# Bias products of the next step's first half issued before the wait for its queries and keys

## What is computed

```python
scores = einsum('bhqd,bhkd->bhqk', q, k) * scale      # 16 heads of 8 features
# attention 0: scores += -log(distances + 1e-9) * abs(distance_scaling)
# attention 1: where(Mask == 0, -1e9, scores)
# attention 2: causal mask
# attention 3: where(mask, scores, -inf), sum + 1e-6 in the softmax
# attention 4 (inside L3_ffn): causal mask over the tokens of a sequence
attn = softmax(scores);  out = einsum('bhqk,bhkd->bhqd', attn, v)
```

## Time and profile before

| | |
|---|---|
| median of 3 runs | 3524.65 us (3519.8 to 3527.03) |
| the profiled execution's own time | 3525.29 us |
| its span, first to last instruction | 3523.3 us |
| TensorE matmul busy | 2743.3 us (78%) |
| VectorE busy | 2155.4 us (61%) |
| ScalarE busy | 1559.4 us (44%) |
| GpSimd busy | 738.0 us (21%) |
| mean granted TensorE clock | 0.906 of full speed |

### The profile page before, as it was taken

One profiled execution on the slowest core, in us unless ns is written; L12 is line 12 of the kernel. 1 busy time (PEld: TensorE's weight loads), 2 busy tenths in 40 slices (PEclk: granted clock), 3 DMA queues, 4 the chain that ended last, 5 costly groups with the idle time before them and its releaser, 6 DMA issues.

```text
span 3523.3 us, 123502 instructions
## 1 busy us (share of the span) xinstructions
PE 2743.3 (78%) x46829; PEld 1889.7 (54%) x46829; DVE 2155.4 (61%) x6318; ACT 1559.4 (44%) x3530; POOL 738.0 (21%) x999
## 2 busy tenths in 40 slices
PE   2888886689898997888889588885488885309994
PEld 1666665466664443666654356653366664206773
DVE  5666667777776776777762476677666665622223
ACT  3444445355554333555554254456544443303331
POOL 1223220133330000000000222221000000774553
PEclk9999896699998998999989799998799997559997
DMA  7223223122223000000000011112200002112214
GB/s 200 70 69 74 66 72 128 31 49 46 48 46 107 0 0 9 10 10 9 10 5 0 14 19 17 18 18 59 63 20 19 20 19 59 49 32 77 70 46 154
DMA packets 247824, 161.41 MB, mean 46 GB/s; under 512 B 135892, under 2 KB 221818, under 8 KB 246662
## 3 DMA queue, kind: packets, MB, share of 16 engines
q1 hardware_dynamic: 238470, 145.67, 16.1%
q0 software_dynamic: 9216, 13.88, 1.2%
HBM read 107.89 MB, written 56.82 MB: 47 GB/s over the span
## 4 chain that ended last, share of the span: by engine, by line
PE 50%; DVE 19%; issue 13%; SPq 5%; DMA 5%; POOL 4%; ACT 2%; DVEq 1%; ACTq 0%; POOLq 0%
PE ps L583 8%; PE ps L526 6%; DVE negmax L1304 6%; PE ps L728 5%; PE ps L531 5%; PE ps L850 4%; PE ps L860 4%; DVE qk L1285 4%; DMA ffb<-b_dram 4%; POOL slots L1836 3%; PE ps L569 3%; PE ps L603 3%; PE ps L506 2%; SPq L361 2%; DVE rec L1336 2%
## 5 line engine op out<-in xcount | busy, mean ns | idle before, releaser
L1304 DVE TENSOR_REDUCE negmax<-ps 128x4 f32<-128x480 f32 (+1 forms) x1280 | 790.1, 659 | 459.5 <-PE ps L531 443.5
L938 ACT ACTIVATE ex<-ps 120x1024 f32<-120x1024 f32 (+1 forms) x640 | 659.9, 1033 | 371.5 <-PE ps L569 371.5
L1787 POOL TENSOR_SCALAR ffb<-ffb 128x480 bf16<-128x480 int32 (+1 forms) x128 | 232.5, 1816 | 688.0 <-PE ps L569 563.5
L559 PE MATMUL ps<-qk 32*120 32x128 f32 (+1 forms) x10240 | 362.2, 280 | 0.0
L583 PE MATMUL ps<-ex,vpad 120*32 120x128 f32 (+1 forms) x10240 | 358.7, 282 | 2.4 <-issue 1.5
L923 ACT COPY mT<-ps 128x128 bf16<-128x128 bf16 x320 | 85.1, 266 | 581.5 <-PE ps L537 581.5
L559 PEld LDWEIGHTS ps<-qk 32*120 32x120 f32 (+1 forms) x10240 | 316.7, 186 | 0.0
L583 PEld LDWEIGHTS ps<-ex,vpad 120*32 120x32 f32 (+1 forms) x10240 | 269.1, 112 | 57.8 <-issue 54.2
L526 PE MATMUL ps<-ffb,identb 32*32 32x480 bf16 x3072 | 154.9, 379 | 144.8 <-DMA ffb<-b_dram 60.4
L1836 POOL DMA_INDIRECT slots<-xw,slot_of x128 | 132.0, 1031 | 619.8 <-DVEq L1682 578.4
L1285 DVE SCALAR_TENSOR_TENSOR qk<-ps,cols,cpack 128x480 f32<-128x480 f32 (+1 forms) x320 | 228.7, 715 | 40.1 <-ACT qk L917 40.1
(11 more groups left out here) (242 smaller groups left out, 5169.6 us busy)
## 6 DMA issues: line engine op xcount, KB each, us to landing
ffb<-b_dram SPq DMA_DIRECT2D x256, 90.0 KB, 2.4
ctxT<-in_ctxT SPq DMA_DIRECT2D x256, 60.0 KB, 1.8
ffb<-in_mask SPq DMA_DIRECT2D x256, 60.0 KB, 2.0
slots<-xw SPq DMA_DIRECT2D x1, 10560.0 KB, 31.1
h_all<-slots SPq DMA_DIRECT2D x40, 264.0 KB, 2.8
z<-xw SPq DMA_DIRECT2D x1, 8192.0 KB, 24.6
b_dram<-bparts SPq DMA_DIRECT2D x64, 90.0 KB, 1.9
w_sb<-in_L_W SPq DMA_DIRECT2D x2, 2048.0 KB, 10.2
```

Source lines behind the costliest of these rows:

```text
L559: pe.matmul(bank(g)[:, k * P:(k + 1) * P], kblk[of, j, k * nk:(k + 1) * nk], qs[of, j, :], start=False, stop=False, skip_group_check=True)
L938: act.activation(ex[0:nk, j, c * 1024:(c + 1) * 1024], b_ps[c][0:nk, :], ACT.Exp).then_inc(S["e_ready"], 1)
L1304: dve.tensor_reduce(negmax[:, j, HG * g:HG * g + HG], a_ps[g % 2][:, 0:HG * nk].rearrange("p (a n) -> p a n", a=HG), AX.X, ALU.max, negate ...
L1787: pool.tensor_scalar(mask4[:, j, :, :].rearrange("p c n -> p (c n)"), raw[:, j, :, :].rearrange("p c n -> p (c n)"), 0.0, MASKED, ALU.is_e ...
```

## The change

In `scores_by_query`, half 0, the waits for queries and keys are taken from the top and placed between the bias products (L526) and the products of queries and keys (L531), with an increment of `pe_step` of their own behind them. The bias products then wait only for the bias (stages 0, 1, 3) and for the banks. Nothing else is changed: the order of products, half 1 and all other engines stay.

```diff
                     if half == 0:
-                        pe.wait_ge(S["q_ready"], nth("q_ready", s, i))
-                        pe.wait_ge(S["k_ready"], nth("k_ready", s, i))
                         if s in (1, 3):
                             pe.wait_ge(S["bias_ready"], nth("bias_ready", s, i))
                         if s == 0:
...
                             pe.matmul(a_ps[c][32 * m:32 * m + 32, 0:HG * nk], identb[of, of], bc(bias4(j)[of, m, :], HG),
                                       start=True, stop=False, skip_group_check=True)
+                    if half == 0:
+                        pe.wait_ge(S["q_ready"], nth("q_ready", s, i))
+                        pe.wait_ge(S["k_ready"], nth("k_ready", s, i))
+                        pe.sem_inc(S["pe_step"], 1)
                     for c in range(2):
                         g = 2 * half + c
                         of = slice(g * 32, g * 32 + 32)
```

## The result

The changed kernel takes 3381.84 us, the median of 4 runs (3372.61 to 3388.23); the kernel before took 3525.84 us beside it (3519.8 to 3533.65). The ratio is 0.9588, with a 95% interval of 0.9554 to 0.9622: 144 us, or 4.1%, less. A second set of 4 runs gave 3381.79 us and a ratio of 0.957 (0.9541 to 0.9599).

A forecast was written before the change was run, and what follows sets the result against it. The prediction took a TensorE-VectorE loop through the keys as the bound. Gains of 104.2 us in the looped steps of stages 1 to 4 and 6 in written-out steps made 110: 3525.3 - 110 = 3415 us, range 3386 to 3452.

The forecast's parts named there:

- What bounds the kernel: Stage 2's step: a TensorE-VectorE loop through the keys (L1285), bias products (L526) and scores (L531), 6.48 us long.
- first three terms: Stage 2: TensorE from L531 to half 1's L531, 2.63 us; to the maxima, 0.42; VectorE to the keys' end, 2.75.
- The products are hidden: Stages 1 to 4: eight bias products run behind L1285's last third, taking 0.32 us a step off the loop.
- What is left behind the keys: Stages 1 to 4: keys' end to scores, after the change, taken as 0.23 us, bounded by 0.10 and 0.36.
- second loop: Stage 2: leaves VectorE at L1338, passes L537, bias products and scores; put at 5.92 us after the change.
- What is late next: Stage 2 after the change: the loop through the keys, 6.03 us, stays longest, 0.11 before the other binds.
- rival (b): Wait and increment as fast as in written-out steps, so the loop through L1338 binds at 5.92: 3390 us; chance 0.13.
- Stage 0: Bound by the bias DMA, not the keys: no gain taken, with +12 and -6 us kept as possible.
- (a): Only the products are hidden; as many sequencer steps stay behind the keys: 79 us gain, 3446 us; chance 0.15.
- (c): Handing over bias products is slow without sequencer lead, 0.40 us for eight: gain 0.28 a step, 3461 us; chance 0.05.
- (d): No change, as L569's wait for the copied maxima takes over at once: 3525 us; chance 0.03.
- (e): Slower: the sequencer reaches L577 late, and TensorE runs dry before L489 and L583: 3539 us; chance 0.04.

The follow-up runs named there:

- the kernel with the wait last: Kernel before, with half 0's waits for queries and keys, plus their own increment, put last ahead of the bias products: 3485.4 us, ratio 0.9862.
- with its queue mended: Kernel before, with stage 0's bias loads issued on the SyncE queue ahead of the wait for `project_v`: 3475.66 us, ratio 0.9863.

## Why the prediction was right in its mechanism and 33 us short

**What bounds the kernel: right.** The loop over the keys closed before and after. Its first three terms are the same to the hundredth, and only the two that the change was to shorten did change.

**The products are hidden: right.** The bias products run beside the keys (L524 at 1571.97, the keys' end at 1572.21), and that is worth 0.32 a step (6.23 to 5.91 between the kernel with the wait last and the changed one).

**What is left behind the keys: the term that was mis-sized.** The step that failed is "I take 0.23 in all four stages". It measures 0.10 in stages 1, 2 and 4 (856.46 to 856.56 in the rows below, 1572.21 to 1572.31 above) and 0.17 in the median step of stage 3. I had subtracted one sequencer step from three, as if the wait for the keys and the new increment were two. They are one event, L529, which carries both waits and the increment, and the sequencer's rows show no register computation between it and the bias products. So nothing is left behind the keys, and the lower bound of the prediction was the value. Nor do I find anything for the little that I took off for the weight load of L531: bias products in the earlier trace rows and scores here both start 0.10 behind the keys. A step of stage 1 and one of stage 3, after:

```profile
855.75 0.71 DVE L1287 SCALAR_TENSOR_TENSOR qk<-ps,cols,cpack 128x480 f32<-128x480 f32 x1
...
856.56 0.39 PE L533 MATMUL ps<-qk 32*128 32x480 bf16 x2
...
2207.20 0.29 DVE L1340 TENSOR_TENSOR qk<-ps,rec 128x128 f32<-128x128 f32 x1
2207.41 0.71 DVE L1287 SCALAR_TENSOR_TENSOR qk<-ps,cols,cpack 128x480 f32<-128x480 f32 x1
...
2207.62 0.23 PE L539 MATMUL ps<-identb,mparts 128*128 128x128 bf16 x1 [0.38 <-DVE qk L1340]
...
2207.97 0.40 PE L524 MATMUL ps<-ffb,identb 32*32 32x480 bf16 x8
...
2208.30 0.38 PE L533 MATMUL ps<-qk 32*128 32x480 bf16 x2
```

In stage 3 the second loop binds: L539 and L524 are 0.35 apart there, with the mask's wait between them, against 0.16 in stage 2, and the keys, done at 2208.12, wait for the bias.

**What is late next: right, but reached.** The second loop was put at 5.92 and measures 5.90. The first was put at 6.03, with 0.11 to spare, and is 5.90 too. That is rival (b), to which I had given 0.13, with the 5.92 at 3390 us. It was 8 us high: it has the loops but not the clock (below).

**The sum.** The median step went from 6.44 to 5.91 in stage 1, 6.48 to 5.91 in stage 2, 6.55 to 5.96 in stage 3 and 6.64 to 6.05 in stage 4. Over the 56 steps of each loop that is 56 x (0.53 + 0.57 + 0.59 + 0.59) = 128 us, where 104 were predicted. The steps that are written out went down by 0.32 or 0.33 (6.22 to 5.90, in stage 4 6.38 to 6.05), where 0.30 was predicted: 6 us. That is 134 of the 138 us of stages 1 to 4. So 24 of the 33 us that the forecast was short are the mis-sized term, 128 us in place of 104, and the next paragraph has the rest.

**The clock: left out, wrongly.** Stages 3 and 4 went down by 42 and 37 us, but 56 x 0.59 + 1.6 is only 35. The rest is time at half the granted clock, in single steps in mid-stage of the kernel before. Windows over stages 3 and 4 of the kernel before and over one such step in each:

```profile
2006.00:2428.00 422.00, 353.84 (x7911) 253.55 (x7903) 298.41 (x813) 213.51 (x437) 112.58 (x62) 0.98 0.14 27
2515.00:2940.00 425.00, 377.87 (x8075) 264.13 (x8075) 290.99 (x688) 200.01 (x436) 0.00 (x0) 0.98 0.08 19
2124.00:2132.00 8.00, 7.84 (x121) 5.87 (x125) 4.76 (x13) 3.26 (x6) 1.82 (x1) 0.60 0.10 15
2636.00:2644.00 8.00, 8.00 (x123) 5.84 (x125) 4.64 (x11) 2.85 (x5) 0.00 (x0) 0.60 0.07 18
```

and over the same two stages after:

```profile
1949.00:2328.00 379.00, 346.35 (x7891) 247.77 (x7885) 298.00 (x812) 212.79 (x436) 112.57 (x62) 1.00 0.15 30
2416.00:2804.00 388.00, 374.51 (x8083) 265.03 (x8075) 291.24 (x688) 199.96 (x437) 0.00 (x0) 0.99 0.09 21
```

In the steps with 0.60 part of the time is granted 1.2 GHz in place of 2.4, and a step takes 7.9 to 8.9 us. In the kernel before such steps cost 6.9 us in stage 3 and 3.5 in stage 4, 10 us in all. They are in all three profiles of the old form (the kernel before twice, and with its queue mended). The two profiles of the changed kernel have none away from the first steps of a stage, and nor have stages 3 and 4 of any kernel made from it. With these 10 the parts come to 144, 6 more than the 138. Nearly all of that is in stage 1, which shortened by 25 us in the first profile and 29 in the second, where 31 are counted: the first profile began stage 1 at half the clock (0.51 in the window shown with the result). With the stages of the second profile (1523.9 us) the gain in stages 1 to 4 is 143.8.

**Stage 0: right.** It took 470.7 us before and 470.8 after. L524 still waits there for the DMA, 67.5 us over 57 times.

**The other rivals** fall by rows already shown. (a) The scores are 0.10 behind the keys, not 0.36. (c) L524 to L533 takes 0.33 with the sequencer given no lead. (d) L571 waits for the copy 5 times, 1.8 us in all, since the copy (1572.06 + 0.27) ends 0.06 ahead of L571. (e) L579 is reached at 1572.8 and L489 still starts 1.09 after L533.

**What stays open.** Why the granted clock falls in stage 0 and in single steps of the old form is not shown. Before a fall TensorE had been idle: in the old form 0.57 to 0.71 us at a stretch, at the wait for the keys in stages 3 and 4, and in the kernel before 1.2 to 2.7 us, mostly at a DMA, at the falls inside stage 0. The sum of its idle time does not tell the stages apart. In stage 4 of the kernel before it is 47 of 425 us (425.00 - 377.87 above), with such steps; in stage 3 of the kernel with the wait last it is 50 of 398, with stretches of 0.37 at most in its usual step, and without them. No kernel here changed the idle time alone.

A step below 5.90 would need both loops cut at once. The transposes of L539 put behind the bias products might do that, and it wasn't tried. How much it could give is open too, since TensorE itself is nearly full: by the windows above it is busy for 374.51 of 388 us in stage 4, and in the usual step of stage 2 it is idle for 0.08 us. These busy times rest on modelled ends that overlap, so the room that is left is not known.

## What to carry to other kernels

Count what stands between the last arrival and the first instruction that needs it: products that need none of it can go ahead of the wait, and so can the other waits with their register computations. Then the last waits and the increment are one event with nothing behind it. Close the second loop with the same care as the first, and take its length as the bound if the unknown term may be at its lower end. Where an edit that works elsewhere gives nothing in a stage, look for a DMA queue with a wait ahead of the issue that is needed: moving four loads past one wait was worth 75 us, and let the edit pay 24 us in that stage too. Compare stages and not totals where the granted clock varies: two kernels with the same program in stage 0 differed there by 13 to 17 us.

## What was not expected of the hardware

- An increment of a semaphore that stands alone costs 0.15 us on TensorE's path (scores 0.10, 0.25 and 0.40 behind the keys with none, one and two more), while its own row says 51 ns. Two waits and an increment fused in one event cost nothing beyond the 0.10 from the arrival to the first product.
- Eight products of 32x32 by 480 columns and their hand-over take 0.33 us with the sequencer given no lead, no longer than with a lead (0.32 to 0.34).
- In the middle of a regular loop the granted clock falls to 0.60 over single steps, in stages where TensorE is idle for no longer than 0.57 to 0.71 us at a stretch, in three profiles out of three of that form.
- The length of stage 0 is 457 to 508 us as its mean granted clock goes from 0.99 to 0.87, and length times clock stays at 442 to 452 us. Two increments behind the keys do not show in that product, only in the clock.
